# Attention over 4096 nodes: SyncE issues its half of a unit's exchange ahead of the row load that waits for the unit before

## The reference, cut to what matters

```python
h = maximum(layernorm(x), 0)                       # x: 4096 x 256, fp32
q, k, v = h @ Wq.T + bq, h @ Wk.T + bk, h @ Wv.T + bv
a = q @ k.T / sqrt(256) + adj + adj                # adj: 4096 x 4096, fp32
out = x + softmax(a, axis=-1) @ v
```

## Time and profile before

| | us |
|---|---|
| median of 3 runs | 740.02 |
| lowest, highest | 736.87, 742.82 |
| profiled execution | 735.11 |
| its span | 733.4 |
| TensorE busy in the span | 693.4 (95%) |
| VectorE busy | 599.9 (82%) |
| ScalarE, GpSimd busy | 436.7 (60%), 433.7 (59%) |

### The profile page before, as it was taken

How to read it: one execution, slowest core, us unless ns; L and a number is a source line. 1 busy time by engine, 2 the same in 40 slices (tenths; PEclk the granted TensorE clock), 3 DMA queues, 4 the chain that set the end, 5 groups by cost and what they waited for, 6 DMA issues and landing times.

```text
span 733.4 us, 14700 instructions
## 1 busy us (share of the span) xinstructions
PE 693.4 (95%) x4799; PEld 473.1 (65%) x4799; DVE 599.9 (82%) x1282; ACT 436.7 (60%) x732; POOL 433.7 (59%) x436
## 2 busy tenths in 40 slices
PE   5588998999999999999999989999999999999988
PEld 4455554566666676766666756666666666666776
DVE  4889776789797879788888869787877888897996
ACT  3799662675656665656666565656575566656530
POOL 1789602565655657474756555564747475655667
PEclk7699999999999999999999999999999999999999
DMA  8298597998988888899989979899999999998573
GB/s 267 102 264 242 148 225 215 256 239 242 237 217 240 230 224 221 222 220 248 230 230 222 228 207 244 221 228 236 211 229 245 227 224 242 235 228 228 148 179 81
DMA packets 93244, 161.06 MB, mean 220 GB/s; under 512 B 20976, under 2 KB 41840, under 8 KB 93168
## 3 DMA queue, kind: packets, MB, share of 16 engines
q1 hardware_dynamic: 68432, 126.41, 65.7%
q10 hardware_dynamic: 24736, 33.72, 18.8%
HBM read 80.35 MB, written 8.39 MB: 121 GB/s over the span
## 4 chain that ended last, share of the span: by engine, by line
PE 50%; DMA 18%; SPq 16%; DVE 8%; issue 4%; ACT 2%; POOL 1%; ACTq 0%; DVEq 0%; POOLq 0%
PE bank L1442 28%; PE bank L1503 21%; SPq L420 13%; DMA xT<-rows 8%; DMA out_y<-xy 4%; DMA g_pair<-g_scratch 2%; DMA rows<-in_x 2%; SPq L372 1%; DVE rows L1127 1%; DMA v_sb<-xT 1%; DVE rows L1100 1%; SPq L409 1%; DMA rows<-in_adj 1%; DVE stats L1045 1%; DVE top L1136 1%
## 5 line engine op out<-in xcount | busy, mean ns | idle before, releaser
L624 POOL TENSOR_TENSOR wT<-xT,wT 128x512 f16<-128x512 f32 x233 | 268.9, 1165 | 216.7 <-ACT wT L806 213.2
L1442 PE MATMUL bank<-v_sb,wT 128*128 128x256 f16 x2796 | 344.8, 273 | 7.8 <-POOL wT L624 4.5
L1503 PE MATMUL bank<-top,a_op 128*128 128x512 f16 x1344 | 331.5, 380 | 7.3 <-DVE rows L1078 3.5
L1442 PEld LDWEIGHTS bank<-v_sb,wT 128*128 128x128 f16 x2796 | 273.2, 98 | 91.3 <-POOL wT L624 6.5
L806 ACT CAST wT<-xT 128x512 f16<-128x512 f32 x233 | 139.6, 612 | 133.6 <-PE bank L1442 78.0
L1503 PEld LDWEIGHTS bank<-top,a_op 128*128 128x128 f16 x1344 | 130.5, 98 | 118.5 <-DVE rows L1078 5.0
L777 ACT ACTIVATE rows<-rows,exp_bias,exp_scale 128x1024 f32<-128x1024 f32 x128 | 158.7, 1240 | 59.4 <-issue 30.8
L1100 DVE CUSTOM_DVE_ANT_0 rows<-bank,rows 128x512 f32<-128x512 f32 x256 | 173.5, 680 | 10.3 <-PE bank L1503 2.0
L1127 DVE STREAM_TRANSPOSE rows<-rows 128x1024 f32<-128x1024 f32 x128 | 158.3, 1239 | 8.8 <-ACT rows L777 8.7
L1085 DVE SCALAR_TENSOR_TENSOR rows<-rows,adj_scale,bank 128x512 f32<-128x512 f32 x64 | 47.7, 745 | 40.5 <-PE bank L1503 40.5
L1078 DVE SCALAR_TENSOR_TENSOR rows<-rows,adj_scale,bank 128x512 f32<-128x512 f32 x64 | 47.5, 742 | 31.3 <-PE bank L1503 15.7
(11 more groups left out here) (115 smaller groups left out, 479.3 us busy)
## 6 DMA issues: line engine op xcount, KB each, us to landing
rows<-in_adj SPq DMA_DIRECT2D x128, 512.0 KB, 5.7
xT<-rows SPq DMA_DIRECT2D x488, 64.0 KB, 3.8
xT<-rows ACTq DMA_DIRECT2D x488, 64.0 KB, 4.3
rows<-in_x SPq DMA_DIRECT2D x8, 512.0 KB, 6.0
xy<-in_x SPq DMA_DIRECT2D x32, 128.0 KB, 4.7
g_scratch<-xT SPq DMA_DIRECT2D x16, 256.0 KB, 3.1
g_pair<-g_scratch SPq DMA_DIRECT2D x15, 256.0 KB, 5.7
out_y<-xy SPq DMA_DIRECT2D x30, 128.0 KB, 5.4
```

Source lines behind the costliest of these rows:

```text
L624: nc.gpsimd.tensor_tensor(split_piece(m, 1), exchanged(m), split_piece(m, 0), ALU.subtract).then_inc(split_lo, 1)
L1442: return nc.tensor.matmul(out_ap, stationary, moving, start=first, stop=last)
L1503: last = nc.tensor.matmul(ps[:], s, mv, start=first and k == 0, stop=k == 2, skip_group_check=True)
```

## The change

In the loop `period(n)` of SyncE, `exchange_a(u)` is put ahead of `refill(u - 1, 0)` and of `load_g(p + 1)`; it stood behind both. Nothing else changes: not the waits inside these functions, not the hand-written order of SyncE up to period 6, no other engine. `exchange_a(u)` brings its 8 DMAs along and its waits for `turned` and for the low parts of unit u - 3.

```diff
             def period(n):
                 p, u = n // QUADS, n - EXP_LAG
+                if unit_in_range(u):
+                    exchange_a(u)
                 if unit_in_range(u - 1):
                     refill(u - 1, 0)
                 if n % QUADS == 0 and p + 1 < PAIRS:
                     load_g(p + 1)
-                if unit_in_range(u):
-                    exchange_a(u)
                 if unit_in_range(u - 1):
                     refill(u - 1, 1)
                 if n % QUADS in (2, 3) and p >= 2:
```

## The result

| | before | changed |
|---|---|---|
| median of 20 runs, us | 739.93 | 729.41 |
| lowest, highest | 727.87, 748.82 | 726.05, 733.02 |
| profiled execution, its span | 735.11, 733.4 | 730.58, 728.8 |

The change makes the kernel faster, by 0.8%: the ratio is 0.9922 with an interval of 0.9899 to 0.9944. That ratio leaves out runs over 1.5% above the fastest of their kernel, 13 of the 20 of the kernel before and none of the changed one; over all runs the medians stand at 0.986. The two numbers differ because the spread has changed as well: 21 us before, 7 us after.

A forecast was written before the change was run, and what follows sets the result against it. SyncE's round, nearly as long as TensorE's, was taken to make loads late: 735.1 - 7.6 + 2.0 + 0.3 = 729.8 us, plus half of the 4.9 us up to the median, gave 732 us; range 727.5 to 742.

The forecast's parts named there:

- The stock and the levels: TensorE's 7.6 us of waits as all that could be gained; half of the 4.9 us from profile to median given back.
- the sum against the profiled execution: Whole kernel: 735.1 - 7.6 us of TensorE waits + 2.0 + 0.3 us of new costs = 729.8 us.
- The working of the round: SyncE's four periods: issues and waits 37.6 us, falling to about 31, against TensorE's 39 to 40 us.
- The tight place: SyncE, once a round: the store's landing frees the second `load_xy` late, so unit 4k's exchange starts 2.6 us late.
- The even exchange: Rival: stores land near 13.2, late `load_g` costs 13 rounds 0.45 us each, 6 us for 7.6; 738 us, chance 0.25.
- One sign of being wrong: In SyncE's loop: `load_g` landing more than 5.7 us after the end of the next unit's part 0 transposition.
- The new cost: TensorE waiting behind later `load_g` landings: 0.15 us as the mean of 13 rounds, 2.0 us.
- The limit of 5.66 us: `load_g` costs TensorE time once it lands over 5.66 us after the next unit's part 0 transposition ends.
- The 0.3 us for late row loads at `scores_11`: Periods 4p: row load lands at 13.4, wanted at 13.98, costs from 15.0; 0.3 us over all rounds.
- The slower rival: `load_g` behind the previous period's store lands at 6.9 us, costing 16 us for 7.6; about 748 us, chance 0.13.
- price of 13 us for each 1 us: Every 1 us by which `load_g` lands later costs 13 us over the kernel, no round spared.
- The rule weighed: Skill's DMA fit, 2 us plus bytes at 436 GB/s: refills delay no store, sum 727.5 us; chance 0.05.

The follow-up runs named there:

- The old order with a shorter round: Against the kernel before, both `load_xy` loads moved from period 4p + 3 to the end of period 4p + 4 (also called `load_xy` later): 727.95 us.
- The half-loop kernel: Against the kernel before, `exchange_a(u)` put first only up to period 31, old order from period 32: 733.49 us.
- `load_g` last: Against the changed kernel, `load_g` moved behind the second refill, `refill(u - 1, 1)`: 750.96 us.

## Why the prediction was right

*The stock and the levels.* 732 us was predicted, 729.41 measured, inside the range. The part that was worked out from rows is the sum against the profiled execution: 729.8 us, and it took 730.58. The step that was mis-sized is the last: of the 4.9 us between the first profile of the kernel before and its median I gave back half. All of it went, and more: the changed kernel's median lies 1.2 us below its own profile. This term was a guess, and that the sum came so close is in part luck: the second pair of profiles, 734.2 and 731.41 us, is 2.8 us apart and not 4.5. The reason given for the term was that the old order multiplies what varies between executions. The spreads (21 us against 7) agree, but the old order with `load_xy` later spreads by 5 us only, so it is the full round and not the order that does it.

*The cause.* SyncE's round was the bound on the late loads. The old order with a shorter round shows it, in its profile and in its median, and the landing waits that stay there show that they matter only through the round's length. The half-loop kernel shows that it builds up over several periods. The working of the round was short, though: outside the two waits of the earlier trace rows SyncE's queue took (280 - 80.5) / 7 = 28.5 us a round, not 26.1, so the round was 40 us and not 37.6. The same reckoning gives 34.5 us for the changed kernel, with its wait for the store, where about 31 was forecast. That is still below TensorE's 39 to 40, so the conclusion stands.

*The tight place.* (Numbers without a row above are worked out from the same timelines.) I predicted the exchange of unit 4k 2.6 us behind its transposition; it is 3.4 at unit 16, 3.8 at unit 40, 3.3 at unit 56, and the mean of units 8 to 56 is 2.8. The exchange behind it, of unit 4k + 1, was to be on time and is 1.0 us late in the mean, 2.5 at most. The store was to land in 6.5 us after issue; its median is 6.2, of the 1.8 us for a second row load ahead 0.8 came. The even exchange was built on 7.2 us. `load_g` was to go out 1.05 us before the next unit's transposition and is between 1.6 us before and 1.5 us after; but it lands in 4.7 us, not 6.1; why it is quicker was not tested. The later issue in some rounds and the quicker landing nearly cancel. One sign of being wrong did appear: `g_pair` was there more than 5.7 us after the mark in two rounds, at units 37 and 41, and these are the two that paid.

*The new cost.* 2.0 us were put down for late `g_pair` in 13 rounds; two rounds paid, 0.77 and 1.81 us, 2.6 in all. The limit of 5.66 us held: the begin of the sums less TensorE's wait is 7.44 - 1.81 = 5.63 in the changed kernel and 9.72 - 4.09 = 5.63 with `load_g` last. GpSimd waited in every round from unit 8 on, as foreseen, for 1.4 to 5.7 us. The 0.3 us for late row loads at `scores_11` measured nothing. TensorE's two waits for `scores_11`, 0.7 us, have no load behind them, and the larger, 0.47 us at 283.27, is there in the old order with `load_xy` later too (0.49 us at 283.06). With another 0.8 us behind `top` this makes 1.5 us of waits that the sum did not have; 1.3 us less busy time nearly made up for them.

*The range's other side.* The slower rival was real: with 0.5 us and 512 KB in front of `load_g` it happens, 751 us. Its price of 13 us for each 1 us held for the waits: the sums began 7.3 us after the mark in the mean of 13 rounds, 1.65 us past the limit, which is 21.5 us by that price, and 21.5 us of waits were measured. What it did not have is the clock. The profiled execution is 23.5 us longer than that of the changed kernel, of which some 18.9 us are more waits for GpSimd's low parts; the lower clock after the two longest waits is about 3.4 us more, an estimate from 8 us at 0.57 to 0.62 and 4 us at 0.95.

*The rule weighed.* The Trainium skill (DMA: Bandwidth & Descriptors, "Anatomy of one DMA — SWDGE (gpsimd) path") fits 2 us and the bytes at 436 GB/s to a DMA of GpSimd's path; for a store of 128 KB this is an estimate of 2.3 us, with no term for what runs beside it. SyncE's stores do not agree: 5.4 us with one row load ahead and 6.2 with two. (The "near 2.6" of the prediction's sentence on this rule is the duration of `load_g` by the fit; by an estimate with its issue some 3.6 us ahead of the mark, it would land 1 us ahead of it.)

*Not settled.* No execution of the kernel before above 740 us was profiled. That the 10 us and more which it then has over the changed kernel are slides that start early is not shown: the kernel with the new order from period 32, whose runs reach 16 us above its fastest, fits it, but the second profile of the kernel before slid from unit 16 on and lost no more than the first. What is shown is that they go with SyncE's full round, in whichever way it is shortened.

## What to carry to other kernels

Where one in-order queue issues the loads for all, add up its round, issues and waits, and compare it with the bound engine's round: if they are equal, small losses add up and show only far from their origin, and the time scatters. Put ahead what waits for an event of the present period and behind it what waits for the last period's landing, but check for every instruction moved back when its reader needs it: one load issued 0.7 us later, behind 512 KB more, turned this gain of 1.4% into a loss.

## What the runs showed of the hardware

Here a small DMA landed about when the larger ones issued just before it on the same queue did. By the pages' medians, the output stores of 128 KB took 4.9 to 5.7 us in the five profiles with one row load just ahead, and 6.0 to 6.3 us in the seven with two. `g_pair`'s 256 KB landed in 3.4 to 4.0 us where no row load stood just ahead of it (behind 8 exchange DMAs, or behind the wait for a store's landing), in 4.6 to 5.7 us behind one and in 6.4 to 7.3 us behind two. It is not the place in the order alone: `load_g` ahead of the exchange has 3.7 us where SyncE had just waited for a store, and 7.2 us with `load_xy` later, where it had just issued two row loads and a store.

TensorE's granted clock stayed at 1.00 after waits of up to 1.9 us, and was 0.57 and 0.62 for some 4 us after waits of 4.09 and 4.33 us.

The DMA engines' busy share fell from 0.92 to 0.86 in the loop's second part, with the same bytes and packets over the kernel: so the packets themselves took less time; why was not tested. It is no cause of the gain, since the old order with a shorter round has 0.90 and the same speed.
